# Two edits to a graph-network kernel: where the first layer's gather waits, and how segment maxima are finished

## The reference, cut to what matters

```python
q = h @ Wq + bq;  k = h @ Wk + bk;  v = h @ Wv + bv        # per node
logits = sum(q[dst] * k[src], axis=-1) * 8 ** -0.5 + edge_attr   # per edge and head
seg_max = segment_max(logits, dst)
ex = exp(logits - seg_max[dst])
attn = ex / (segment_sum(ex, dst) + 1e-16)
out = segment_sum(v[src] * attn, dst)                      # per node
x = x + out @ Wo + bo
```

## Time and profile before

| | |
|---|---|
| three runs | 3136.4, 3146.5, 3149.1 us, median 3146.5 |
| the profiled execution | 3114.8 us |
| its span, first to last instruction | 3112.8 us |
| mean granted TensorE clock | 0.651 |
| busy share of the span | PE 67%, DVE 57%, POOL 55%, ACT 36% |

### The profile page before, as it was taken

How to read it: one execution, slowest core, us unless ns; L and a number is a source line. 1 busy time by engine, 2 the same in 40 slices (tenths; PEclk the granted TensorE clock), 3 DMA queues, 4 the chain that set the end, 5 groups by cost and what they waited for, 6 DMA issues and landing times.

```text
span 3112.8 us, 40117 instructions
## 1 busy us (share of the span) xinstructions
PE 2081.3 (67%) x10636; PEld 1720.0 (55%) x10636; DVE 1767.0 (57%) x6156; ACT 1134.2 (36%) x3023; POOL 1714.8 (55%) x1755
## 2 busy tenths in 40 slices
PE   6876767664355655551895777777786777777775
PEld 4544444443233333330783777677774677767775
DVE  9766656565467776558983444444446444343445
ACT  8433333331145445441123333333333333333331
POOL 1566666665666666660002666666662666666661
PEclk7555555555577777785897766666666666566665
DMA  2000000003222222230002333333333333333332
GB/s 76 4 5 4 5 4 4 4 5 102 70 60 66 65 64 67 65 54 3 1 1 98 111 109 112 109 109 113 111 107 81 111 109 110 110 108 112 109 105 32
DMA packets 114126, 209.58 MB, mean 67 GB/s; under 512 B 46139, under 2 KB 57213, under 8 KB 113533
## 3 DMA queue, kind: packets, MB, share of 16 engines
q0 software_dynamic: 69632, 146.42, 17.0%
q1 hardware_dynamic: 44284, 60.61, 6.3%
HBM read 193.30 MB, written 13.60 MB: 66 GB/s over the span
## 4 chain that ended last, share of the span: by engine, by line
another core or an unknown queue 20%; DVE 17%; PE 11%; issue 9%; ACT 3%; POOL 1%; DMA 1%; DVEq 0%; ACTq 0%; POOLq 0%
PE PS L1165 4%; DVE work L1319 4%; DVE red L1324 4%; DVE work L1336 3%; DVE work L1311 2%; PE PS L1393 2%; ACT kv L747 2%; PE PS L1403 2%; POOL arena L1299 1%; DMA arena<-kv_d,S 1%; DVE work L738 1%; PE PS L759 1%; PE PS L1405 1%; PE PS L1250 1%
## 5 line engine op out<-in xcount | busy, mean ns | idle before, releaser
L1299 POOL DMA_INDIRECT arena<-kv_d,S x528 | 512.4, 970 | 281.4 <-issue 151.2
L1403 PE MATMUL PS<-work,R 128*128 128x128 f32 x1760 | 560.5, 413 | 56.2 <-issue 49.3
L1299 POOL DMA_INDIRECT kv<-kv_d,S x352 | 343.0, 975 | 423.5 <-DMA kv_d<-arena 249.1
L924 POOL DMA_INDIRECT kv<-kv_d,S x440 | 425.1, 966 | 258.0 <-issue 132.7
L664 POOL DMA_INDIRECT sorted_d<-S,rows x416 | 419.4, 1008 | 265.9 <-issue 172.6
L1393 PE MATMUL PS<-arena,work 128*128 x1760 | 397.5, 397 | 241.6 <-DVE work L1319 206.5
L1393 PEld LDWEIGHTS PS<-arena,work 128*128 128x128 f32 x1760 | 343.6, 290 | 259.8 <-issue 259.8
L1360 ACT ACTIVATE R<-iota,gate 128x128 f32<-128x128 f32 x880 | 280.0, 388 | 445.8 <-remote 333.8
L1403 PEld LDWEIGHTS PS<-work,R 128*128 128x128 f32 x1760 | 406.2, 281 | 60.2 <-issue 59.5
L1405 PEld LDWEIGHTS PS<-wts,R 128*128 128x128 f32 x1760 | 401.1, 278 | 55.5 <-issue 55.5
L759 PE MATMUL PS<-kv,work 128*128 128x440 f16 x832 | 232.5, 440 | 243.8 <-DVE work L738 169.0
(11 more groups left out here) (269 smaller groups left out, 3173.8 us busy)
## 6 DMA issues: line engine op xcount, KB each, us to landing
work<-segT_d SPq DMA_DIRECT2D x165, 256.0 KB
kv<-kv_d,S POOLq DMA_INDIRECT x792
arena<-kv_d,S POOLq DMA_INDIRECT x528
sorted_d<-S,rows POOLq DMA_INDIRECT x416
kv_d<-arena SPq DMA_DIRECT2D x12, 512.0 KB, 2.9
sorted_d<-S SPq DMA_DIRECT2D x1, 2200.0 KB, 8.0
S<-sorted_d SPq DMA_DIRECT2D x1, 2040.0 KB
work<-in_edge_attr_dram SPq DMA_DIRECT2D x1, 1660.0 KB
```

The source lines that it names most:

```text
L924: gp.indirect_dma_start(out=kv_near[:, g % SLOTS, j, :], out_offset=None, in_=kv0_d, in_offset=bass.IndirectOffsetOnAxis(ap=S0[:, t, 1:2]. ...
L1299: gp.indirect_dma_start(out=ring[s][:, j, :], out_offset=None, in_=kv1_d[l], in_offset=bass.IndirectOffsetOnAxis(ap=S1[:, t, 1:2], axis=0) ...
L1403: nc.tensor.matmul(PS[:, ds(blocks[g % 3][j] * DM, DM)], R[:, s, j, :], vw[:, n % 3, j, :], start=False, stop=True, skip_group_check=True)
```

## The change

In stage A, the third transfer of each group (j = 2) additionally waits until the queries of the group two before it have been expanded. In the maxima, the carries from both sides are put into `fwd` alone; the second round does all eight forward scans first and then all eight backward scans over their results, so that `bwd` alone holds the full maximum and the instruction on line 1097 falls away; the logits are shifted in four pieces (tiles 0 to 63, 64 to 191, 192 to 319, 320 to 439), ScalarE takes the exponential of each as it comes, and stage B waits for the piece that its group lies in.

```diff
+PIECES = [(0, 64), (64, 192), (192, 320), (320, T)]
...
                 for j in range(TG):
                     t = g * TG + j
+                    if j == TG // 2:
+                        since(gp, s_qe0, g - SLOTS + 3)
                     gp.indirect_dma_start(
...
-        def runs(source_f, source_b):
-            for h in range(H0):
-                nc.vector.tensor_tensor_scan(fwd[:, h, 1:T + 1], gate0[:, 0:T], source_f[:, h, :], -BIG, ALU.min,
-                                             ALU.max)
-                done = nc.vector.tensor_tensor_scan(bwd[:, h, T:0:-1], gate0[:, T:0:-1], source_b[:, h, ::-1], -BIG,
-                                                    ALU.min, ALU.max)
-            vstep(done)
+        def forward(h, source):
+            return nc.vector.tensor_tensor_scan(fwd[:, h, 1:T + 1], gate0[:, 0:T], source[:, h, :], -BIG, ALU.min,
+                                                ALU.max)
+
+        def backward(h, source):
+            return nc.vector.tensor_tensor_scan(bwd[:, h, T:0:-1], gate0[:, T:0:-1], source[:, h, ::-1], -BIG,
+                                                ALU.min, ALU.max)
...
-            runs(LGT, LGT)
+            for h in range(H0):
+                forward(h, LGT)
+                done = backward(h, LGT)
+            vstep(done)
...
-            for b in range(NB):
-                at = fwd[:, 0:H0, ds(places0[b] + 1, 1)]
-                vlag(nc.vector.tensor_tensor(at, at, into[:, 0, :, b:b + 1], ALU.max))
-                at = bwd[:, 0:H0, ds(places0[b + 1], 1)]
-                vlag(nc.vector.tensor_tensor(at, at, into[:, 1, :, b:b + 1], ALU.max))
+            for b in range(NB + 2):
+                if b < NB:
+                    at = fwd[:, 0:H0, ds(places0[b] + 1, 1)]
+                    begins = nc.vector.tensor_tensor(at, at, into[:, 0, :, b:b + 1], ALU.max)
+                    if b < 2:
+                        vstep(begins)
+                    else:
+                        vlag(begins)
+                if b >= 2:
+                    at = fwd[:, 0:H0, ds(places0[b - 1], 1)]
+                    vlag(nc.vector.tensor_tensor(at, at, into[:, 1, :, b - 2:b - 1], ALU.max))
             dve.wait_ge(s_v, vcount[0])
-            runs(fwd[:, :, 1:T + 1], bwd[:, :, 1:T + 1])
-            vstep(nc.vector.tensor_tensor(fwd[:, 0:H0, 1:T + 1], fwd[:, 0:H0, 1:T + 1],
-                                          bwd[:, 0:H0, 1:T + 1], ALU.max))
-            nc.vector.tensor_tensor(LGT, LGT, fwd[:, 0:H0, 1:T + 1], ALU.subtract).then_inc(s_shift, 1)
+            for h in range(H0):
+                done = forward(h, fwd[:, :, 1:T + 1])
+            vstep(done)
+            for h in range(H0):
+                done = backward(h, fwd[:, :, 1:T + 1])
+            vstep(done)
+            for lo, hi in PIECES:
+                nc.vector.tensor_tensor(LGT[:, :, lo:hi], LGT[:, :, lo:hi], bwd[:, 0:H0, lo + 1:hi + 1],
+                                        ALU.subtract).then_inc(s_shift, 1)
+            dve.wait_ge(s_shift, len(PIECES))
...
-            act.wait_ge(s_shift, 1)
-            at = S0[:, :, 2:W0P]
-            nc.scalar.activation(at, at, ACT.Exp).then_inc(s_ex, 1)
-            act.wait_ge(s_ex, 1)
+            for n, (lo, hi) in enumerate(PIECES):
+                act.wait_ge(s_shift, n + 1)
+                at = S0[:, lo:hi, 2:W0P]
+                nc.scalar.activation(at, at, ACT.Exp).then_inc(s_ex, 1)
...
-            dve.wait_ge(s_ex, 1)
...
                 since(dve, s_sum0, g - 1)
+                dve.wait_ge(s_ex, 1 + sum(hi < (g + 1) * TG for lo, hi in PIECES))
...
                 since(act, s_sum0, g - 1)
+                act.wait_ge(s_ex, 1 + sum(hi < (g + 1) * TG for lo, hi in PIECES))
```

## The result

| | before | after |
|---|---|---|
| median of four runs each, one chip | 3147.1 us | 3110.4 us |
| lowest and highest | 3136.4 to 3149.1 | 3102.0 to 3112.4 |
| ratio, 95% interval | | 0.9891 [0.9866, 0.9916] |
| profiled execution, its span | 3114.8, 3112.8 | 3102.0, 3100.0 |

The medians differ by 36.7 us; the ratio, which is not that of the two medians, gives 34 (26 to 42 by its interval). The two profiled executions differ by only 12.8: up to the end of stage B, which the change touches, after is 30.6 us shorter (before: from 730.90 to 1618.74; after: from 738.47 to 1595.73), while the unchanged rest took 17.8 longer in the one execution than in the other (7.6 ahead of stage A, 10.2 behind B). Stages are therefore compared here, not spans.

A forecast was written before the change was run, and what follows sets the result against it. Stage A was taken as bound by GpSimd's serial gather, 82% full, plus its pauses. Stage A -25 + 4 = -21 and maxima -6.5 gave -27.5 us, the median 3119.0; range 3088 to 3150, likeliest 3105 to 3131.

The forecast's parts named there:

- The cycle: Stage A: TensorE's results come out late while GpSimd issues transfers; GpSimd's waits cost 112.3 us in 37 pauses.
- Pauses shortened: Stage A's gather: a pause ends when queries appear, not after product or copy; mean of bursts of 12 and 8, -25 us.
- bursts of 8: Stage A's gather: pauses after every eight transfers, 55 x 1.75 = 96 us, 16 less than 112.3.
- The line through four cases: Stage A: a pause lasts about 0.7 us plus 0.125 us per transfer of the burst, estimated from bursts of 4, 8, 12, 24.
- The start: Start of stage A: group 3's third transfer waits for group 1's queries, so group 4 starts 4 us later.
- The end of stage A: Last groups of stage A: a chain from the last queries, the same as before, so no change.
- Maxima: Maxima to B's first matmul: line 1097 gone -3.86, exponential in pieces -2.9, added waits +0.3; together -6.5 us.
- The signs: Expected profile: old gather waits nearly gone, TensorE waits near 87 us, products 0.1 us behind the resumed gather, stage lengths.
- Bursts of four: Rival, stage A: every third transfer finds its queries missing, pauses cost +21 us; 3165 us in all, chance 0.13.
- Nothing in stage A: Rival: TensorE is late by itself, so stage A gains 0 and only the maxima's -6.5 remain; 3140 us, chance 0.23.
- Much faster: Rival, stage A: the gather, never far ahead, lets TensorE out without pausing or rarely; 3101 or 3088 us, chance 0.14.
- The maxima were not eaten: Rival, maxima and B: lost covers of memset and extra waits give +0.3 in place of -6.5; 3126 us.

The follow-up runs named there:

- the fourth chip: The changed kernel and two variants of its wait, run on another chip, where the kernel before takes 2738.2 us; the changed kernel's ratio was 0.9985.

## Why the prediction was right

Forecast 3119.0 us (-27.5), measured 3110.4 (-36.7). Direction and size hold, and the maxima's share was met for its reasons. That stage A came out near its forecast is in part luck: two errors in it cancel.

- **The cycle** (GpSimd waits for a product, the product for queries, the queries for GpSimd to stop) is shown: with the gather's transfers gone, or made by SyncE, no product waits for queries and TensorE's signals come at once, and in the pauses of before and after they come late and in bunches. It is a fact of the chips with 3110 to 3157 us, not of the kernel: on the fourth it doesn't exist. The Trainium skill's rule in "SBUF — State Buffer", section "Who interferes with whom", that TensorE never waits on anyone for SBUF and DMA doesn't contend with engines, would have made the stage's gain 0. On the fourth chip the whole gain of 4.1 us agrees with that. On the others it does not, though no run says that SBUF has a part in it, which is what the rule is about.
- **Pauses shortened, forecast -25**: the idle time between transfers fell by 16.2 with the start's +2.9 in it, so the pauses gave 19. This is the mis-sized step. The pauses are nearly as many as "bursts of 8" has, 52 (gaps over 0.5 us between transfers, counted in the timeline), but they last 2.13 us each, not 1.75. After a burst of 8 they last 1.65 (26 of them), after 12 2.58 (9), but after 4 2.22 (13) where I had 1.21. The line through four cases was too thin, and it left something out: in 9 of these 13 pauses the queries' own matmuls end, by the model, only 1.0 to 4.6 us after the burst. There the gather waits for TensorE's work, not for a held signal. It is so in 12 of the 52 pauses. Before there were 41 of 3.01.
- **The start, forecast +4**: +2.9.
- **The end of stage A, forecast 0**: -9.6, the step that was wrong. I took the chain from the last queries as given, but the number of groups left at the end of the gather is the lead, and the wait cuts it, four products to two. In the other kernels with the wait, on the chips that hold signals, the end is 4.6 to 15.2 us shorter than the 21.8 of before; up to 3.7 of that also appears without the wait. Gather and end together: -24.0, forecast -21.
- **Maxima, forecast -6.5**: -6.66. From the start of the maxima to the first subtraction 55.84 us for 59.55; from there to the first matmul 8.42 (8.5 forecast) for 11.37. The memset cost nothing, and stage B takes 125.1 us for 125.0.
- **The signs.** The gather's waits for products and copies are nearly gone (1.8 and 1.2 us). Their successors were to add up to near 87 us and add up to 110.4 in the view (67.0 + 43.4), which counts the usual 0.30 us ahead of a transfer in wherever it names a releaser; the whole idle time, 228.8 for 245.0, is the fairer measure. The product was to follow the resumed gather by 0.1 us; in 41 of the 52 pauses it precedes it, by 0.18. So the gather does not resume ahead of the product, but 0.5 us sooner behind it than the 0.69 of before.
- **The sum** in the profiles up to the end of B: -30.6. The median's further 6 us lie within its interval; nothing was found for them.
- **Rivals.** Bursts of four came 13 times, between bursts of 8 and 12, and not throughout; the reason that the rival gave for them (the next queries are not out) holds in 9. Nothing in stage A holds on the fourth chip, where the whole change gives 4.1 us. Its chance of 0.23 was thought of as a mechanism, and turned out as a chance of chips. Much faster did not come: 52 pauses stayed. The maxima were not eaten.

**Open.** Why the fourth chip doesn't hold signals. The changed kernel's stages without transfers by GpSimd are as long there as on the first chip (maxima 64.2 and 64.3 us, stage B 124.5 and 125.1), and those with them are 12% to 13% shorter: the sort's 416 transfers 560.2 us for 633.9, stage A 582.4 for 667.9, the second part from its first transfer 1245.8 for 1438.3. No profile of the kernel before was taken there. Where a signal stands between TensorE and the semaphore isn't seen in any row.

## What to carry to other kernels

Where an idle consumer starts work just after a serial engine falls silent, let that engine wait for the event that the consumer misses, and not for the consumer: it ends each pause earlier and cuts the lead, which is paid for at the end of the stage. Of several such waits that do as well, the weakest is the one to try first: its start costs less (group 4 began 25.7 us after the first transfer, not 30.2, on the fourth chip), and the gain depends on the chip. And measure a gain that rests on waits between engines on more than one chip; transfers and products agreed here within 1% in duration while the kernel before took 12% to 13% less on one chip.

## What the runs showed of the hardware

- On the chips with 3110 to 3157 us, TensorE's semaphore updates come late while GpSimd issues indirect transfers back to back: 22 of 95 on time in the kernel before, and in one pause four of them 0.09 us apart, 4.7 to 9.2 us behind the model's ends. The gather stands still for 111 us of a stage of 692 beyond its pitch. Transfers of the same size and consecutive rows issued by SyncE, at 85 GB/s in all, leave them on time (110 of 110).
- VectorE's and ScalarE's recorded updates in the same stage are on time: 72 of 72 for the products, 62 of 62 for the copies, within 0.02 us.
- One chip does without: its transfers keep the same pitch (0.30 us between them), all 110 updates of `s_qe0` come 0.014 or 0.015 us behind the matmuls' modelled end, most of them in the middle of a run of 426 transfers, and the kernel before takes 2738 us.
- Chips that show the holding differ among themselves by 1.5% on one kernel (3110.2 and 3157.1).
